# The last stage's first product moved from GpSimd to VectorE for two of eight feature tiles

## The reference

```python
# x: (8, 4096, 1024) float32
xn = _layernorm(x, axis=-1)
s = attention(xn, W_kqv)              # 16 heads, ALiBi bias, softmax
g = _silu(ffn(xn, ...))               # 3 cycles of out += coupling * twist(out)
x = x + s * g
```

## Time and profile before

| what | us |
|---|---|
| median of 2 timed runs | 2819.58 (2793.37 and 2845.79) |
| the profiled execution | 2787.24 |
| its span, slowest core (core 6) | 2785.7 |
| spans of the 8 cores | 2770.6 to 2785.7 |
| last stage on core 6, from the last update of `STATE` to the end | about 2506.7 to 2785.7 |
| PE, DVE, ACT, POOL busy over the whole span | 2224.5, 809.3, 1470.1, 102.5 |

### The profile page before, as it was taken

One profiled execution on the slowest core, in us unless ns is written; L12 is line 12 of the kernel. 1 busy time (PEld: TensorE's weight loads), 2 busy tenths in 40 slices (PEclk: granted clock), 3 DMA queues, 4 the chain that ended last, 5 costly groups with the idle time before them and its releaser, 6 DMA issues.

```text
span 2785.7 us, 34009 instructions; the slowest of 8 cores (2770.6 to 2785.7 us)
## 1 busy us (share of the span) xinstructions
PE 2224.5 (80%) x9380; PEld 911.0 (33%) x9380; DVE 809.3 (29%) x1342; ACT 1470.1 (53%) x2366; POOL 102.5 (4%) x150
## 2 busy tenths in 40 slices
PE   0238879899999988899888855788888888865998
PEld 0233324233333333333222215433333333322443
DVE  1554432211010011000000006344335435445333
ACT  0222466677788988999999950233333333324000
POOL 1000000000000000000000000000000000002333
PEclk9668989999998999999999975899999999985555
DMA  9611111000000000000000024544444444424665
GB/s 190 167 31 31 36 27 24 8 16 16 1 9 9 9 9 9 9 1 9 9 9 9 8 57 166 134 109 99 102 107 110 95 112 105 98 67 134 205 209 181
DMA packets 343980, 190.30 MB, mean 68 GB/s; under 512 B 303419, under 2 KB 321981, under 8 KB 343694
## 3 DMA queue, kind: packets, MB, share of 16 engines
q1 hardware_dynamic: 323470, 160.08, 21.9%
q0 software_dynamic: 3696, 11.27, 2.8%
q10 hardware_dynamic: 16640, 16.78, 2.1%
HBM read 165.30 MB, written 36.96 MB: 73 GB/s over the span
## 4 chain that ended last, share of the span: by engine, by line
PE 55%; ACT 14%; DVE 13%; issue 10%; DVEq 4%; DMA 3%; ACTq 1%; SPq 0%; another core or an unknown queue 0%; POOL 0%; POOLq 0%
PE PA L693 13%; ACT PBUF L454 12%; PE PC L446 5%; PE PA L446 5%; PE PA L378 3%; PE PD L428 3%; PE PC L378 3%; PE PBp L428 3%; PE PD L430 3%; PE PBp L892 3%; DVE STATE L809 2%; DVE TMP L800 2%; DVE SBF L778 2%; PE PA L892 2%; PE PC L867 2%
## 5 line engine op out<-in xcount | busy, mean ns | idle before, releaser
L454 ACT ACTIVATE PBUF<-PC,ebias_s 128x512 bf16<-128x512 f32 x979 | 657.3, 754 | 145.3 <-PE PC L446 97.2
L454 ACT ACTIVATE PBUF<-PA,ebias_s 128x512 bf16<-128x512 f32 x965 | 648.1, 752 | 145.6 <-PE PA L446 76.5
L446 PE MATMUL PC<-QT,KT 64*128 64x512 bf16 x979 | 346.6, 387 | 64.8 <-ACT PBUF L454 46.4
L693 PE MATMUL PA<-SBF,W1S 128*128 128x512 bf16 x1536 | 356.9, 396 | 24.4 <-DVE SBF L778 20.5
L446 PE MATMUL PA<-QT,KT 64*128 64x512 bf16 x965 | 323.7, 390 | 59.9 <-DVE QT L385 25.8
L704 ACT ACTIVATE H<-PA,b1c_s 128x512 bf16<-128x512 f32 x192 | 131.9, 687 | 341.6 <-PE PA L693 341.6
L800 DVE TENSOR_TENSOR TMP<-PD,STATE 128x512 f32<-128x512 f32 x192 | 123.7, 686 | 360.9 <-PE PD L792 355.1
L693 PEld LDWEIGHTS PA<-SBF,W1S 128*128 128x128 bf16 x1536 | 153.8, 101 | 227.6 <-issue 64.4
L428 PE MATMUL PD<-PBUF,VB 128*65 128x512 bf16 x528 | 209.3, 396 | 20.3 <-ACT PBUF L454 11.3
L430 PE MATMUL PD<-PBUF,VB 128*65 128x512 bf16 x528 | 208.3, 395 | 0.0
L726 PE MATMUL PBp<-H,W2S 128*128 128x512 bf16 x768 | 175.2, 378 | 37.5 <-DMA W2S<-w2b_s 34.2
(11 more groups left out here) (103 smaller groups left out, 1892.7 us busy)
## 6 DMA issues: line engine op xcount, KB each, us to landing
W1S<-w1b_s SPq DMA_DIRECT2D x192, 256.0 KB, 2.9
W2S<-w2b_s SPq DMA_DIRECT2D x96, 256.0 KB, 2.9
XTs<-x SPq DMA_DIRECT2D x8, 2048.0 KB, 30.4
sraw_s<-SRW SPq DMA_DIRECT2D x64, 256.0 KB
XT2s<-x SPq DMA_DIRECT2D x16, 1024.0 KB, 5.9
XT<-x SPq DMA_DIRECT2D x32, 512.0 KB, 6.9
SINB<-sraw_s ACTq DMA_DIRECT2D x16, 1024.0 KB, 6.2
out<-OUT SPq DMA_DIRECT2D x32, 512.0 KB, 3.1
```

Source lines behind the costliest of these rows:

```text
L446: inst = TE.matmul(RING[r], lhs, QT[b][hh * 64:(hh + 1) * 64, sc * SC2:(sc + 1) * SC2], start=True, stop=True)
L454: inst = SE.activation(out=PB_[slot][:], in_=RING[r], func=AF.Exp, bias=ebias[:, h * 32 + nt: h * 32 + nt + 1], scale=1.0 / 32.0)
L693: inst = TE.matmul(HALF[slot][:], W1S[wslot][:, ft * 128:(ft + 1) * 128], sbf[:, ft * TC:(ft + 1) * TC], start=(ft == 0), stop=(ft == NF - 1))
```

## The change

Of the 8 tiles of a chunk, tiles 1 and 5 (`VE_FT`) are no longer multiplied by GpSimd. VectorE multiplies `STATE` by `SINB` for them itself, straight into their places in `SG2`, two instructions ahead of the chunk's tile loop, with a `drain` behind them; in the loop it multiplies those two places by the spread reciprocals in place. GpSimd does 6 tiles in place of 8. The wait for the transposes of the chunk before moves ahead of the two new products, and a wait for `SINB` and two for silu are added there. The bookkeeping of the `FTMP` buffers becomes a count of its own. The load of `SINB` waits for VectorE's eighth product of the chunk, besides GpSimd's last.

```diff
@@ -833,13 +833,15 @@
+        ftmp_tok = [0, 0]
...
             if sin_tok[sb6]:
-                SE.wait_ge(gTT1.h, sin_tok[sb6])
+                SE.wait_ge(gTT1.h, sin_tok[sb6][0])
+                SE.wait_ge(vTT2.h, sin_tok[sb6][1])
...
@@ -870,18 +872,30 @@
+            VE_FT = (1, 5)
+            if tch > 0:
+                VE.wait_ge(tTRS.h, 2 * tch)
+            VE.wait_ge(sSIND[sb6].h, sSIND[sb6].n)
+            for ft in VE_FT:
+                VE.wait_ge(sSilu.h, ft + 1)
+                VE.tensor_tensor(out=SG2[0][:, ft * TCF:(ft + 1) * TCF],
+                                 in0=STATE[:, ft * S + tch * TCF: ft * S + tch * TCF + TCF],
+                                 in1=SINB[sb6][:, ft * TCF:(ft + 1) * TCF], op=AOP.mult)
+            VE.drain()
+            gp_i = 0
             for ft in range(NF):
-                b2_ = sg_idx % 2
-                GP.wait_ge(sSIND[sb6].h, sSIND[sb6].n)
-                GP.wait_ge(sSilu.h, ft + 1)
-                if sg_idx >= 2:
-                    GP.wait_ge(vTT2.h, sg_idx - 2 + 1)
...
-                gTT1.inc(inst)
-                if ft == NF - 1:
-                    sin_tok[sb6] = gTT1.n
+                if ft not in VE_FT:
+                    b2_ = gp_i % 2
+                    GP.wait_ge(sSIND[sb6].h, sSIND[sb6].n)
+                    GP.wait_ge(sSilu.h, ft + 1)
+                    if ftmp_tok[b2_]:
+                        GP.wait_ge(vTT2.h, ftmp_tok[b2_])
...
+                    gTT1.inc(inst)
+                    gp_i += 1
...
@@ -893,16 +907,21 @@
-                VE.wait_ge(gTT1.h, gTT1.n)
                 VE.wait_ge(tRDB.h, tRDB.n)
-
-                if tch > 0 and ft == 0:
-                    VE.wait_ge(tTRS.h, 2 * tch)
-                inst = VE.tensor_tensor(out=SG2[0][:, ft * TCF:(ft + 1) * TCF],
-                                        in0=FTMP[b2_][:], in1=HALF[slot][:, 0:TCF], op=AOP.mult)
+                if ft in VE_FT:
+                    inst = VE.tensor_tensor(out=SG2[0][:, ft * TCF:(ft + 1) * TCF],
+                                            in0=SG2[0][:, ft * TCF:(ft + 1) * TCF],
+                                            in1=HALF[slot][:, 0:TCF], op=AOP.mult)
+                else:
+                    VE.wait_ge(gTT1.h, gTT1.n)
...
+                    ftmp_tok[(gp_i - 1) % 2] = vTT2.n + 1
                 vTT2.inc(inst)
                 pxp.append((ft, vTT2.n))
                 sg_idx += 1
+            sin_tok[sb6] = (gTT1.n, vTT2.n)
```

More of the change, by code:

```diff
@@ L871, in flush_xp @@
                         tTRS.inc(inst, 2)
-            for ft in range(NF):
-                b2_ = sg_idx % 2
-                GP.wait_ge(sSIND[sb6].h, sSIND[sb6].n)
-                GP.wait_ge(sSilu.h, ft + 1)
-                if sg_idx >= 2:
-                    GP.wait_ge(vTT2.h, sg_idx - 2 + 1)
-                inst = GP.tensor_tensor(out=FTMP[b2_][:],
-                                        in0=STATE[:, ft * S + tch * TCF: ft * S + tch * TCF + TCF],
-                                        in1=SINB[sb6][:, ft * TCF:(ft + 1) * TCF], op=AOP.mult)
-                gTT1.inc(inst)
-                if ft == NF - 1:
-                    sin_tok[sb6] = gTT1.n
+            VE_FT = (1, 5)
[9 more added lines that the diff above has]
+            gp_i = 0
+            for ft in range(NF):
+                if ft not in VE_FT:
[4 more added lines that the diff above has]
+                        GP.wait_ge(vTT2.h, ftmp_tok[b2_])
+                    inst = GP.tensor_tensor(out=FTMP[b2_][:],
+                                            in0=STATE[:, ft * S + tch * TCF: ft * S + tch * TCF + TCF],
+                                            in1=SINB[sb6][:, ft * TCF:(ft + 1) * TCF], op=AOP.mult)
+                    gTT1.inc(inst)
+                    gp_i += 1
                 slot = sg_idx % 4
@@ L895, in build_program @@
                 flush_xp()
-                VE.wait_ge(gTT1.h, gTT1.n)
                 VE.wait_ge(tRDB.h, tRDB.n)
-                if tch > 0 and ft == 0:
-                    VE.wait_ge(tTRS.h, 2 * tch)
-                inst = VE.tensor_tensor(out=SG2[0][:, ft * TCF:(ft + 1) * TCF],
-                                        in0=FTMP[b2_][:], in1=HALF[slot][:, 0:TCF], op=AOP.mult)
+                if ft in VE_FT:
[4 more added lines that the diff above has]
+                    VE.wait_ge(gTT1.h, gTT1.n)
+                    inst = VE.tensor_tensor(out=SG2[0][:, ft * TCF:(ft + 1) * TCF],
+                                            in0=FTMP[(gp_i - 1) % 2 if ft not in VE_FT else 0][:],
+                                            in1=HALF[slot][:, 0:TCF], op=AOP.mult)
+                    ftmp_tok[(gp_i - 1) % 2] = vTT2.n + 1
                 vTT2.inc(inst)
```

## The result

The changed kernel takes 2811.31 us (median of 11 runs), the kernel before 2794.83 (median of 10, the two runs shown above among them). The ratio is 1.0062, 95% interval 1.0049 to 1.0074: 0.6% slower, which is about 17 us, 14 to 21 by the interval. The 2845.79 among the two runs shown first was a disturbed execution, and it had lifted the median above 2819; the undisturbed runs of before lie between 2790.9 and 2795.6 with a median of 2793.5, and all ratios here compare undisturbed runs with each other. The profiled execution of the changed kernel took 2803.0 us with a span of 2801.5 on core 1, 15.8 more than that of before.

What follows compares the result with a forecast made beforehand. In the last stage PE is all but full, and VectorE sets the end at each turn. Products 0.64, drain 0.16 and waits 0.14 make 0.94 us; 16 places give 15.0, added to 2787.24: 2802.2 us, range 2790 to 2840.

Steps and rivals of the forecast that it cites:

- PE's wait: PE waiting for a VectorE product, 16 times: from 35.1 us to about 50 us.
- the steady tile: One tile in steady work away from the turn, set by PE: stays at 1.77 us.
- the chunk: Time from one turn's product 0 to the next: about 16.1 us, where it was 15.15.
- two products: VectorE's new `STATE` by `SINB` products between second addition and product 0: 0.32 us each, 0.64 per place.
- drain and the two waits behind it: On VectorE ahead of product 0: drain 0.16 us, waits for PE's matmul and POOL's product 0.14 together, per place.
- GpSimd's fewer products: 32 products, 23 us of busy time, removed from an engine nobody waits for in the stage: gain nothing.
- the load of `SINB`: Issued up to 2.7 us later, after VectorE's product 7, yet landing before it is needed: cost nothing.
- collision with GpSimd: Rival: new product meets a GpSimd product at every place, up to 0.72 us each, 11.5 us more, 2814; chance 0.07.
- the base: Time of the kernel before to which the slowdown was added: the profiled execution's 2787.24 us.
- Hidden products: Rival: new products run earlier than placed, or PE catches up within the chunk; not slower, 2787 us; chance 0.05.
- `SINB` late: Rival: the later-issued load lands late at the turn, over 2% slower, 2843 us and more; chance 0.02.
- the brake: Rival: GpSimd's product came last at two tiles per chunk, so removing it gains at most 23 us, 2764; chance 0.02.

Runs made afterwards that it cites:

- four tiles: Changed kernel with VectorE multiplying tiles 1, 3, 5 and 7 ahead of product 0, GpSimd the other four: ratio 1.0100 to the kernel before.
- both runs with all transposes behind: Transposes after the chunk's eighth spreading matmul: kernel before, 0.9779 (2730.25 us); changed kernel with its new products behind product 0, 0.9784 (2733.72 us).
- the first run: Changed kernel with its two new products and their drain moved behind product 0 of the chunk: ratio 0.9996 to the kernel before.
- three tiles behind: Transposes follow their spreading matmul three tiles behind, not one: kernel before with this edit 0.9896, changed kernel with it 0.9891.

## Why the prediction was right or wrong

**What bounds it, and where the change costs: right.** The place (VectorE between the second addition and product 0, 15 turns and one start), PE's wait (50 us forecast, 50.7 in the trace), the steady tile and the chunk (16.1 forecast, 16.20) came as written. The run with the products moved behind product 0 shows that the place is all but some 1 us of it: the same work behind product 0 costs nothing that the times show.

**The terms.** For one place 0.94 us were forecast and 0.95 measured.

| term | forecast | measured | from |
|---|---|---|---|
| two products | 0.64 | 0.66 | the run with the drain moved: 1.80 - 1.14 |
| drain and the two waits behind it | 0.16 + 0.14 | 0.29 to 0.30 | 2.09 - 1.80, and the run without products: 1.44 - 1.14; divided below |
| GpSimd's fewer products | 0 | 0 | four tiles, and both runs with all transposes behind |
| the load of `SINB` | 0 | 0 | that edit alone: 1.0001 |
| collision with GpSimd | 0 | 0 | 0.75 us a pair at the turn; 1.28 and 1.30 where GpSimd met it |

The 0.29 also divides as forecast, which I call an estimate, as no run changed the number of waits alone. The engine's gap behind a drain is 2502.62 - (2501.26 + 1.29) = 0.07 us with no wait behind it, 0.14 and 0.16 with one (2657.13 - (2655.71 + 1.28), and the last row of the run with the drain moved), and 0.21 to 0.23 with two. That is some 0.07 us for each wait, though it is long met, beside the lost overlap of 0.08. The run with the waits in the other order has the same 0.21 us of standing still, so it is not their order.

**What was missed.** I named the waits behind the drain and not those inside the tile loop. There the change also puts the wait for GpSimd behind that for PE, and each such product starts 0.07 us later after its matmul. It lies on PE's path once a chunk, at tile 7, as there is nothing between the transposes of tiles 6 and 7. It is 0.07 to 0.08 us by the run with the order put back, some 1.2 us in 16 chunks. 15.0 + 1.2 is 16.2, against 16.6 from the trace and about 17 from the ratio.

**What was wrong: the base.** The step that failed is "The whole: the profiled execution's 2787.24 (a span of 2785.7 and 1.5 around it) + 15.0 = 2802.2 us": it takes a single execution for the time of the kernel before. Measured, that time is 2794.83, and that of the changed kernel 2811.31. Of the 9.1 us between 2802.2 and 2811.3, 7.6 are this base (2794.83 - 2787.24), and 1.5 the slowdown, 16.5 us where 15.0 were summed. Worse, the table at the head of the document says 2819.58, and 2802 set beside that reads as 0.6% faster, where 0.6% slower was measured. I saw that the two bases differ by 32 us ("on the median the same sum gives 2834.6"), kept the forecast on one and used the other only for the range. Two runs 52 us apart, with the profiled execution beside the lower one, suggested that the upper was the odd one. The mean of the other two, 2790.3, would have given 2805, still 6 under. A sum over a base is a difference, and should be stated as one: +15 us, slower. That the range held 2811 is no merit: from 2790 to 2840 it also held the 2794.8 of the kernel unchanged, and on the forecast's own base a slowdown of over three times 15.

**The rivals.** Hidden products need another place in VectorE's order, which the first run gave them; `SINB` late, the brake and the collision did not occur.

## What to carry to other kernels

Work moved onto an engine that is idle for two thirds of a stage costs nothing in its rests and everything at the one place where the others wait for it, so look for that place in the order of time and put new instructions behind it, not ahead: the same two products and drain cost some 15 us ahead of product 0 and nothing that could be measured behind it. An idle gap of the bound engine at a turn is better closed by giving that engine work in its own order (here: transposes further behind, 1% to 2% faster, though part of this is TensorE's shorter order of work) than by relieving engines that nobody waits for. On the path, a drain costs the overlap of the two instructions around it (0.08 us here), a short standstill (0.07) and some 0.07 for each wait behind it, and of two waits the one that ends last should stand last. And a forecast of a few tenths of a per cent is stated as a difference, as a base of one or two executions can be off by more.

## What the runs showed of the hardware that I had not expected

- A VectorE product with two inputs in SBUF and a GpSimd product that reads SBUF do get in each other's way, at 0.53 to 0.55 us for a pair (1.28 and 1.30 us, against 0.75). In both runs it is VectorE that is late, and GpSimd hardly (0.78 where it takes 0.72 otherwise, and 1.41 for two as otherwise).
- Alternating two kinds of float32 matmul costs time on TensorE: a spreading matmul and a pair of transposes take 1.77 us alternating and 0.94 + 0.43 when each stands among its own kind, all at the granted clock of 0.50. I know this only for these two shapes, and what in the alternation costs was not tested.
- In the stretch with all transposes behind, the granted clock was 0.58 in the mean with PE busy for 88% of the time, while in before it was 0.50 with PE busy for 92%, and with three tiles behind 0.50 with PE busy for 97% (194.54 of 200 us). What let it rise was not tested.
- A semaphore wait that has long been met isn't free behind a drain: VectorE stands for 0.07 us with no wait there, 0.14 to 0.16 with one and 0.21 to 0.23 with two.
